# Clearing four accumulators in HBM from GpSimd's queue instead of ScalarE's

## The reference

```python
xn = layernorm(x)
h = xn @ weight_l
agg = segment_sum(edge_weight[:, None] * h[dst], src, N)        # the edge stage
gnn = agg + bias_l + xn @ weight_r + bias_r
mix = linear attention of xn with a gate computed from a second norm, projected
x = x + gnn + mix
xn2 = layernorm(x)
# 8 experts of 256 -> 512 -> 256, the 2 best per node, weighted by a softmax
x = x + sum over the 2 best experts e of w_e * (gelu(xn2 @ W1[e] + b1[e]) @ W2[e] + b2[e])
```

## Time and profile before

| | |
|---|---|
| median of 3 runs | 4450.23 us (4450.19 to 4452.52) |
| the profiled execution, its own time | 4440.3 us |
| its span, first to last instruction | 4438.6 us |
| set-up, to the start of the edge stage | 62.4 us |
| first indirect add of the edge stage | 157.54 us |
| last one, issued | 3255.59 us |
| busy share of the span: PE, DVE, ACT, POOL | 76%, 56%, 38%, 70% |

### The profile page before, as it was taken

One profiled execution on the slowest core, in us unless ns is written; L12 is line 12 of the kernel. 1 busy time (PEld: TensorE's weight loads), 2 busy tenths in 40 slices (PEclk: granted clock), 3 DMA queues, 4 the chain that ended last, 5 costly groups with the idle time before them and its releaser, 6 DMA issues. The chain is left out here.

```text
span 4438.6 us, 85552 instructions
## 1 busy us (share of the span) xinstructions
PE 3389.3 (76%) x16628; PEld 2802.7 (63%) x16629; DVE 2495.7 (56%) x11386; ACT 1685.6 (38%) x3095; POOL 3111.7 (70%) x2088
## 2 busy tenths in 40 slices
PE   1466666667677677878888888888758859999998
PEld 1355555555565555666666666666557758888887
DVE  3577777665555555666666666666548862222222
ACT  1233333344444443444444444444312224444443
POOL 0488888888888888888888888888855544444444
PEclk7788878788888888888888888888779979999999
DMA  9888888877777777777777777777789965565554
GB/s 380 241 146 155 152 148 147 157 117 118 116 109 115 116 113 114 102 108 108 105 104 107 108 103 105 108 107 102 91 217 296 294 187 143 139 145 141 141 140 114
DMA packets 588869, 638.95 MB, mean 144 GB/s; under 512 B 60524, under 2 KB 553156, under 8 KB 587138
## 3 DMA queue, kind: packets, MB, share of 16 engines
q0 software_dynamic: 279264, 269.84, 48.5%
q1 hardware_dynamic: 262234, 273.19, 20.9%
q10 hardware_dynamic: 47304, 95.18, 5.9%
HBM read 249.82 MB, written 390.09 MB: 144 GB/s over the span
## 5 line engine op out<-in xcount | busy, mean ns | idle before, releaser
L818 POOL DMA_INDIRECT agg<-msg,sidx x1664 | 2585.7, 1554 | 667.5 <-issue 408.7
L1122 PE MATMUL bank<-rows,Cmat 128*128 x3328 | 1025.7, 450 | 166.7 <-ACT msg L1315 140.6
L1315 ACT COPY msg<-bank 128x512 f32<-128x512 f32 x832 | 487.1, 585 | 1486.0 <-DMA agg<-msg,sidx 1209.8
L1122 PEld LDWEIGHTS bank<-rows,Cmat 128*128 128x128 f32 x3328 | 699.1, 224 | 346.7 <-issue 253.8
L873 DVE SCALAR_TENSOR_TENSOR sidx<-seen_sum,trash,srcf 128x4 int32<-128x4 f32 x416 | 92.7, 223 | 1022.8 <-DMA agg<-msg,sidx 1017.6
L2069 POOL DMA_INDIRECT out_dram<-x_y,x_node x210 | 325.7, 1551 | 473.1 <-issue 228.2
L856 DVE TENSOR_SCALAR Emat<-bank,srcf,wtf 128x128 f32<-128x128 f32 x1664 | 564.5, 398 | 0.0
L1106 PEld LDWEIGHTS bank<-Emat,pick 128*128 128x128 f32 x3328 | 518.3, 226 | 41.6 <-issue 17.7
L1106 PE MATMUL bank<-Emat,pick 128*128 128x128 f32 x3328 | 528.7, 311 | 1.6 <-DVE seen L860 1.6
L1097 PE MATMUL bank<-packed,both 128*128 (+1 forms) x416 | 187.3, 451 | 437.9 <-DVE seen L860 427.9
L860 DVE SCALAR_TENSOR_TENSOR seen<-bank,srcf,prior 128x128 f32<-128x128 f32 x1664 | 479.1, 341 | 0.0
(11 more groups left out here) (245 smaller groups left out, 4130.6 us busy)
## 6 DMA issues: line engine op xcount, KB each, us to landing
x_w<-in_L_ffn_W_dram SPq DMA_DIRECT2D x105, 512.0 KB, 4.1
agg<-expert_rows ACTq DMA_DIRECT2D x12, 4224.0 KB, 63.3
r_agg<-agg SPq DMA_DIRECT2D x196, 256.0 KB
x_zin<-table SPq DMA_DIRECT2D x105, 259.0 KB, 4.1
window_raw<-in_x_dram SPq DMA_DIRECT2D x208, 128.0 KB, 2.5
agg<-msg,sidx POOLq DMA_INDIRECT x1664
xn_rows<-n_xn ACTq DMA_DIRECT2D x49, 256.0 KB
xn_turned<-n_xnT ACTq DMA_DIRECT2D x49, 256.0 KB
```

The source lines that it names most:

```text
L818: pool.indirect_dma_start(scratch["agg"][r][:, :], bass.IndirectOffsetOnAxis(ap=sidx[:, j:j + 1], axis=0), msg[:, j % (2 * BATCH), :], Non ...
L1122: mm = nc.tensor.matmul(M[p][:, (q % 2) * D:(q % 2 + 1) * D], Cmat[:, b % 2, q, :], rows[:, bass.ds(slot, 1), :], start=True, stop=True)
L1315: nc.scalar.copy(msg[:, at:at + 2, :].rearrange("p q c -> p (q c)"), M[p][:, :]).then_inc(s_msg, 1)
```

## The change

POOL issues all twelve clears, behind its own last instruction of the set-up; ACT issues none. The constant `READY` and its split go. Sizes, addresses, `zeros` and the count of `s_zeroed` stay.

```diff
-        READY = 7
...
-            act.wait_ge(s_clear, 6)
-            for acc, n in clears[:READY]:
-                act.dma_start(clear_rows(acc, n), zeros).then_inc(s_zeroed, 16)
...
-            for acc, n in clears[READY:]:
-                act.dma_start(clear_rows(acc, n), zeros).then_inc(s_zeroed, 16)
...
             nc.gpsimd.affine_select(out=prior[:], in_=prior[:], compare_op=ALU.is_ge, fill=0.0, base=-1,
                                     pattern=[[-1, P]], channel_multiplier=1).then_inc(s_pool, 1)
+            pool.wait_ge(s_clear, 6)
+            pool.nop(nofuse=True)
+            for acc, n in clears:
+                pool.dma_start(clear_rows(acc, n), zeros).then_inc(s_zeroed, 16)
```

## The result

The change makes the kernel slower by 40.2 us: 4491.23 us median (4487.69 to 4492.63, 4 runs) against 4451.05 (4450.19 to 4452.52), a ratio of 1.0089 with a 95% interval of 1.0071 to 1.0106. The profiled execution took 4490.79 us, its span is 4489.1.

The account below looks back on a forecast made before the run. POOL's first indirect add bounds the kernel: wide at 150 + 24.9 to the edge stage + 26.8 gives 201.7 us against 157.5, +44 us. That makes 4484 us profiled, 4494 us median; range 4445 to 4508.

Parts of the forecast that it names:

- What bounds the kernel: Edge stage: POOL's adds run back to back, 3098.05 us, so the first add's start carries through nearly one for one.
- (1): Set-up: ACT loses its twelve clear issues; the five late ones had cost 2.75 us, so that much is gained.
- (2): Set-up: POOL issues twelve clears from 11.1 us at 1.55 us each, done at 31, no cost before the barrier.
- (3): Set-up loads: ACT's load rows take turns with clear runs, so wide lands at 150 us, not 34.7; bounds 133 to 159.
- (4): wide's landing to edge stage: 24.9 us, edge stage at 175; SP's weights and plan are through earlier, at 135 to 145.
- (5): Edge stage start to first add: now bare instead of hidden under the clears, 26.8 us, first add at 201.7 us.
- (B): Rival at DMA queues: clears give way in short pieces, -12 to 0 us, likeliest -4; chance 0.20, 0.06 for over 0.2% faster.
- (C): Rival at POOL's issue: POOL writes every cut piece itself, first add near 187, +30 us or more; chance 0.08.

Follow-up runs that it names:

- spread_after: The change with load pieces of 124 and 31 rows cut to spread over the 16 DMA engines; +13.5 us against before (1.0033).
- short_spread_free: The change with clear runs of 11 KiB, load pieces cut, and a set-up barrier not waiting for POOL's DMAs; -10.6 us against before (0.9978).
- after_wide: The change with POOL issuing its twelve clears only when all six pieces of wide have landed; +28.6 us against before (1.0069).
- sp_issues: The change with all twelve clears issued early by SP behind its weights in place of POOL; +40.2 us against before (1.0091).
- five_early: The kernel before with only its last five clears moved to POOL early, ACT keeping the first seven; +5.8 us against before (1.0017).
- rows_11k: The change with each clear written as 3 x 128 runs of 11 KiB in place of 128 of 33 KiB; +15.2 us against before (1.0034).
- rows_3k: The change with each clear written as 11 x 128 runs of 3 KiB; +22.2 us against before (1.0051).
- spread_before: The kernel before with load pieces of 124 and 31 rows cut to spread over the DMA engines; -6.0 us (0.9987).
- after_wide_free: after_wide with the set-up's end barrier not waiting for POOL's DMAs; +6.9 us against before (1.0018).
- change_free: The change with only the set-up's end barrier freed from waiting for POOL's DMAs; +39.0 us against before (1.0089).
- spread_free: spread_after with the set-up's end barrier not waiting for POOL's DMAs; +3.4 us against before (1.0011).

## Why the prediction was right

**What bounds the kernel.** Right. In every run the time moved with the first add, to within 2 us in all but spread_after (4.2) and short_spread_free (5.0). Shift of the first add and of the median: 39.7 and 40.2 (the change), 27.3 and 28.6, 39.5 and 40.2, 5.4 and 5.8, 15.2 and 15.2, 23.8 and 22.2, -7.1 and -6.0, 9.3 and 13.5, 8.0 and 6.9, 40.2 and 39.0, 2.9 and 3.4, -5.6 and -10.6, in the order after, after_wide, sp_issues, five_early, rows_11k, rows_3k, spread_before, spread_after, after_wide_free, change_free, spread_free, short_spread_free. From first to last add it took 3101.2 us in place of 3098.05, where I had forecast no change; the thirteen executions spread over 3094 to 3106 us, so these 3 us may be spread.

**(1) ACT's issues.** From the use of `wide` to the edge stage it took 174.04 - 148.47 = 25.6 us; forecast 24.9.

**(2) POOL's issues.** 0.53 us each, not 1.55, and hidden as forecast. But the sentence that they have "no cost by itself" was wrong as a rule. POOL has to be through with the transfers, not with the issues, before the block ends; change_free shows that this was covered in the change, and after_wide that it costs 22 us when it isn't.

**(3) The late `wide`.** Forecast 150, measured 148.5. The mechanism, turns between queues, is confirmed by rows_11k and rows_3k, and by sp_issues for another queue. That the date is met within 2 us is partly luck, since two errors of the sum cancel. The clears were to end at 133 to 137 us and the last landed at 142.6: the first landed at 27.3 (11.7 + 15.6), where the sum has 12.5 + 10.1 = 22.6, and the other eleven took 10.5 us each and not 10.1. Behind them the busiest engine was to need 13 us for 144 rows. The DMA view from 143 to 148 us has 64 packets:

```profile
q10 hardware_dynamic: 64, 0.12, 6.2%
```

So the rest was about half as many rows, and `wide` was used 5.9 us behind the last clear.

The picture of the other engines was wrong as well. I had every engine with 150 to 240 load rows pass 96 of them in turns. The queue rows show 409 packets of ACT's against 509 of POOL's from 24 to 60 us, 162 against 577 from 60 to 100, and 510 against 534 from 100 to 143: for a long stretch the loads did not fill their turns, because ACT's issue stood behind pieces that sit on a few engines. This does not set the date, as sp_issues shows, where ACT's issues ended at 63.8 us and `wide` came no earlier. What was right is that the busiest engine decides, and that its rest comes after the clears: from 143 to 148 us the DMA engines together move 23 GB/s, about one engine's share of the 430 before.

**(4) SP's plan.** Forecast back at 135 to 145 us; its reload was issued from 102.40 us on, well under the chain. It is never the last wait, in spread_free by less than 2 us.

**(5) From the start of the edge stage to the first add.** Forecast 26.8, measured 197.20 - 174.04 = 23.2. The term was 3.6 us too large: the window loads were issued 2.4 us after the start and not 3.6, and the two were out 2.6 us after that and not 4.0. That is 2.7 of the 3.6 us; SP's own steps had been slower while the clears ran. The rest was not traced.

**The rivals.** (B) asked for clears that give way. rows_11k and rows_3k made them give way, and `wide` did come early, at 101 and 70 us. The kernel was still slower by 15 and 22 us, because the barrier waits for POOL's transfers, in rows_3k for a twelfth clear that was issued only at 144.74. So the other side of my forecast rested on a wait that I did not know of: had the clears gone out in short pieces by themselves, the outcome would have been slower too, and not -4 us. The 6% for faster were too many. Nor did the clears of the change come in the packets of at most 4096 B on which this rival leaned: POOL's 577 packets from 60 to 100 us carried 17.34 MB, about 30 KB each. (C) did not come: 0.53 us for 128 runs.

The 9 to 17 descriptors per turn of the Trainium skill (DMA: Bandwidth & Descriptors, Queues, rings and completion order) fit no run here: in the change 28 load rows of 512 bytes passed in the seven turns from 69 to 77.9 us, four a turn for all engines together, and a clear's packets held at most two runs, those of 3 KiB. The Trainium skill (DMA: Bandwidth & Descriptors, Issuing engines are not separate DMA queues) says that the DMAs of different engines run on the same 16 DMA engines and interleave there; sp_issues against the change agrees, 147.9 and 148.5 us.

One slip: I gave L318 as the line where the changed kernel uses `wide`; it is L316.

## What to carry to other kernels

A transfer that nobody needs soon still costs if it runs on another queue than short loads that somebody does need: while it lasts, each of their rows waits for one of its runs. Put it behind them on their own queue, or cut its runs short, and cut the loads so that no piece sits on one DMA engine, which was worth 6 us in the kernel before (0.9987, 0.9978 to 0.9996). Before moving long DMAs to POOL, look at the end of the block: by default it waits for them, which it did not do for ACT's.

## What the runs showed of the hardware that I had not expected

- The end of a block waits for the DMAs that POOL issued. The edge stage began 0.5 to 1.0 us behind the landing of POOL's last clear in four runs (after_wide 161.2 and 162.1, spread_after 142.9 and 143.9, rows_11k 149.2 and 150.1, rows_3k 157.8 and 158.3 us), and without that wait at 61.9 (after_wide_free).
- Behind pieces whose rows do not divide over 16 engines an issue can hold its engine long, beside long runs on another queue: ACT's four issues of the 31 rows and of the 20 numbers behind them took 13 to 36 us each in the change, against 0.5 to 1.7 us for three of the same in the kernel before and 5.61 for the fourth. With the pieces cut, each took 0.6 us or less in spread_after.
- The clears' runs of 3 KiB went in packets of 6.0 KB on average, two runs each; those of 11 and 33 KiB in packets of 10.8 and 30 KB on average (those under 512 B counted in), one each.
- POOL could have eleven clears of 1408 runs outstanding, but not the twelfth, and stood still for 121 us.
- POOL's issue of a plain DMA of 128 runs took 0.53 us, a third of its indirect one of 128 rows (1.55 us).
